# Two-layer adapter and mixture kernel: first layer in steps of two groups, expert numbers read two slots ahead

## What is computed

```python
# layer 0: per batch a 64x64 mixing matrix, then a router over 8 experts of rank 16, the best two
z = einsum('bct,bcd->bdt', x, W0[id0])                 # mixes the 64 rows of a batch
w = top-2 gates of softmax(z @ router_w.T + router_b)  # 8 experts
x = x + einsum('ner,eor->no', (z @ A.T) * w, Bm) * 0.5
# layer 1: per batch one of 16 adapters (1024x1024), a base product, 16 experts of rank 64, the best two
y = einsum('bij,bkj->bik', x, W1[id1])
x = x + y @ base_w.T + base_b + 0.5 * sum_e gate_e * (y @ A1.T) @ B1[e].T
```

## Time and profile before

| | us |
|---|---|
| median of three runs | 1165.05 (1164.32 to 1165.34) |
| the profiled execution | 1167.17 |
| its span | 1165.6 |
| PE busy in it | 1103.1 (95%) |
| DVE busy | 686.3 (59%) |
| ACT busy | 505.3 (43%) |
| POOL busy | 222.2 (19%) |

### The profile page before, as it was taken

One profiled execution on the slowest core, in us unless ns is written; L12 is line 12 of the kernel. 1 busy time (PEld: TensorE's weight loads), 2 busy tenths in 40 slices (PEclk: granted clock), 3 DMA queues, 4 the chain that ended last, 5 costly groups with the idle time before them and its releaser, 6 DMA issues.

```text
span 1165.6 us, 22333 instructions
## 1 busy us (share of the span) xinstructions
PE 1103.1 (95%) x5801; PEld 916.3 (79%) x5802; DVE 686.3 (59%) x1321; ACT 505.3 (43%) x1027; POOL 222.2 (19%) x354
## 2 busy tenths in 40 slices
PE   4899979999999899999999999999999999999998
PEld 4899967878778687878878878767777778888886
DVE  4788943563755637463565486834455366566666
ACT  1012213563745637453565462134555444444443
POOL 1111110020201102010111000054545232223210
PEclk9899979999999899999999999999999999999999
DMA  6499765493765729475665432169999899999995
GB/s 212 169 313 326 258 223 177 136 323 114 256 222 195 266 82 325 153 259 180 221 221 183 137 102 88 57 223 330 345 336 334 315 404 341 348 354 337 324 323 204
DMA packets 114925, 283.11 MB, mean 243 GB/s; under 512 B 17202, under 2 KB 22322, under 8 KB 112946
## 3 DMA queue, kind: packets, MB, share of 16 engines
q1 hardware_dynamic: 85232, 178.95, 43.3%
q0 software_dynamic: 29216, 102.91, 26.0%
q10 hardware_dynamic: 418, 0.53, 0.2%
HBM read 181.65 MB, written 100.70 MB: 242 GB/s over the span
## 4 chain that ended last, share of the span: by engine, by line
PE 74%; DVE 11%; issue 4%; DMA 4%; ACT 3%; DVEq 1%; SPq 1%; ACTq 1%; POOL 0%; POOLq 0%; another core or an unknown queue 0%
PE psum L1439 18%; PE psum L1441 17%; PE psum L1440 17%; PE psum L1533 3%; PE psum L1637 3%; PE psum L1636 3%; PE psum L1525 2%; PE psum L1645 2%; DVE x1g L1045 2%; PE psum L1534 2%; PE psum L1551 2%; PE psum L1553 1%; DMA xp<-act_scratch 1%; PE psum L1449 1%; ACT w L821 1%
## 5 line engine op out<-in xcount | busy, mean ns | idle before, releaser
L1439 PE MATMUL psum<-base_hi,xp_hi 128*128 128x512 f32 x512 | 207.6, 405 | 6.2 <-DVE xp_lo L1177 3.4
L1441 PE MATMUL psum<-base_hi,xp_lo 128*128 128x512 f32 x512 | 200.4, 391 | 0.0
L1440 PE MATMUL psum<-base_lo,xp_hi 128*128 128x512 f32 x512 | 200.2, 391 | 0.0
L1439 PE MATMUL psum<-w,xp_hi 128*128 128x512 f32 x448 | 182.8, 408 | 6.3 <-DVE xp_lo L1095 3.2
L1441 PE MATMUL psum<-w,xp_lo 128*128 128x512 f32 x448 | 177.7, 397 | 0.0
L1440 PE MATMUL psum<-w,xp_hi 128*128 128x512 f32 x448 | 177.3, 396 | 0.0
L1077 DVE TENSOR_TENSOR w<-raw,w 128x1024 fp32r<-128x1024 f32 x112 | 132.4, 1221 | 29.5 <-ACT w L758 23.6
L639 POOL DMA_DIRECT2D raw<-w1T x112 | 59.4, 530 | 442.8 <-DVE w L1077 417.5
L803 ACT ACTIVATE xp_hi<-xp 128x256 fp32r<-128x256 f32 x124 | 51.6, 418 | 183.1 <-PE psum L1441 152.3
L1439 PEld LDWEIGHTS psum<-base_hi,xp_hi 128*128 128x128 f32 x512 | 96.2, 188 | 39.8 <-issue 15.6
L1177 DVE TENSOR_TENSOR xp_lo<-xp,xp_hi 128x256 fp32r<-128x256 f32 x124 | 51.9, 424 | 119.3 <-ACT xp_hi L803 96.5
(11 more groups left out here) (278 smaller groups left out, 1993.5 us busy)
## 6 DMA issues: line engine op xcount, KB each, us to landing
raw<-w1T POOLq DMA_DIRECT2D x120, 512.0 KB, 5.6
delta_scratch<-dl SPq DMA_DIRECT2D x80, 512.0 KB
xp<-act_scratch SPq DMA_DIRECT2D x74, 256.0 KB, 3.3
act_scratch<-yT SPq DMA_DIRECT2D x72, 256.0 KB, 2.2
act_scratch<-x1g SPq DMA_DIRECT2D x16, 1024.0 KB, 5.3
x1t<-act_scratch SPq DMA_DIRECT2D x64, 256.0 KB
out<-x1t SPq DMA_DIRECT2D x62, 256.0 KB
xg<-xT SPq DMA_DIRECT2D x15, 1024.0 KB, 8.6
```

The costliest lines, as they stand in the source:

```text
L1439: mm(out, a_hi, b_hi, start=start, stop=False, skip_group_check=True)
L1440: mm(out, a_hi, b_lo, start=False, stop=False, skip_group_check=True)
L1441: return mm(out, a_lo, b_hi, start=False, stop=stop, skip_group_check=True)
```

## The change

Groups are taken in steps of two (`NS` = 8 steps). `gates0(n)` does both groups of a step in one chain of 17 instructions on tensors twice as wide, and then four products into `hw0`; the y products have two banks (1 and 7), so the index tables move to bank 6; the ring of x has six places, two of them in memory that the second layer uses later. PE, ACT and SP are written out without loops. SP loads `w0tab` behind the first group and ahead of the second (before: ACT, after the first half of the first group had landed). `index_3`, `index_sums(4)` and a new `index_read` (three reads of bank 6) run before the first gates, the rest of `index_4` behind them. In the last steps gates, turns and adds are ordered by hand. POOL waits for 12 groups of `x1_added` before it loads the first pair. The expert numbers are multiplied by `D` on DVE, bounded there alone, and read two slots ahead.

```diff
@@ SP
             sp.dma_start(xg[0][:, ks, :], xT[0, :, ks, :]).then_inc(xg_first[q], 16)
+            for h in range(2):
+                sp.dma_start(w0tab[h * C:(h + 1) * C, :], w0).then_inc(w0_in, 16)
             load_x(1, 1)
@@ POOL
             pool.wait_ge(const_split, 2)
+            pool.wait_ge(x1_added, 4 * (2 * XRING))
@@ ACT
+            def two_groups(n):
+                act.wait_ge(shift0, n + 1)
+                act.activation(sm[:, 1, :, :], sm[:, 0, :, :], ACT.Exp).then_inc(exp0, 1)
+                act.wait_ge(h0T_done, n + 1)
+                for k in range(2):
+                    g = 2 * n + k
+                    if n > 0:
+                        act.wait_ge(o_done, 4 * (g - 2) + 4)
                     ...
+                    act.activation(h0_hi[:, rows_of_g], h0T_of(g), ACT.Copy).then_inc(h0_hi_done, 1)
             z_copy(0)
             ...
-            group0(0)
-            ...
-            with act.Fori(1, NG - KC - 1) as g:
-                group0(g)
+            z_copy(1)
+            z_copy(2)
+            for n in range(NS):
+                two_groups(n)
+                ...
+                for k in range(2):
+                    if 2 * n + 3 + k < NG:
+                        z_copy(2 * n + 3 + k)
+                    if n < NS - 1 and NS - 5 <= n:
+                        w_high(2 * (n - NS + 5) + k, 16)
@@ DVE
+            index_3()
+            index_read()
             gates0(0)
+            for n in range(NS - 1):
+                hidden_low(2 * n)
+                hidden_low(2 * n + 1)
+                if n == 0:
+                    index_4()
+                else:
+                    add_x(2 * n - 1, 1)
+                if n == NS - 2:
+                    gates0(n + 1)
+                add_x(2 * n, 0)
+                add_x(2 * n, 1)
+                ...
+                if n < NS - 2:
+                    gates0(n + 1)
+                    add_x(2 * n + 1, 0)
+                if NS - 5 <= n < NS - 2:
+                    w_low(0, 2 * (n - NS + 5))
+                    w_low(0, 2 * (n - NS + 5) + 1)
+            hidden_low(NG - 2)
+            add_x(NG - 3, 0)
+            add_x(NG - 3, 1)
+            hidden_low(NG - 1)
+            w_low(0, KC - 2)
+            add_x(NG - 2, 0)
+            add_x(NG - 2, 1)
+            w_low(0, KC - 1)
+            add_x(NG - 1, 0)
+            add_x(NG - 1, 1)
@@ PE
+            def two_groups(n):
+                if n < NS - 1:
+                    turn_h0(n)
+                    z_of(2 * n + 3, 0)
+                    y_of(2 * n + 2)
+                    z_of(2 * n + 3, 1)
+                    ...
+                    y_of(2 * n + 3)
+                expand(2 * n)
+                if n == NS - 2:
+                    turn_h0(n + 1)
+                expand(2 * n + 1)
+                if n < NS - 2:
+                    z_of(2 * n + 4, 0)
+                    z_of(2 * n + 4, 1)
             ...
             index_sums(3)
+            z_of(1, 0)
+            y_of(0)
+            index_sums(4)
+            z_of(1, 1)
+            y_of(1)
+            z_of(2, 0)
+            z_of(2, 1)
+            for n in range(NS):
+                two_groups(n)
@@ experts
-                return pe.value_load(etab[0:1, s:s + 1], min_val=0, max_val=E1 - 1)
+                return nc.values_load(etab[0:1, s:s + 1], engines=[mybir.EngineType.PE], min_val=0,
+                                      max_val=(E1 - 1) * D,
+                                      skip_runtime_bounds_check_because="VectorE bounds every entry to 15 * D")
-                    m = experts[:, bass.ds(e * D + h * 512, 512)]
+                    m = experts[:, bass.ds(e + h * 512, 512)]
-            e = expert_of(0)
+            ahead = [expert_of(0), expert_of(1)]
             for s in range(NX):
-                expert(s, e)
-                if s + 1 < NX:
-                    e = expert_of(s + 1)
+                expert(s, ahead.pop(0))
+                if s + 2 < NX:
+                    ahead.append(expert_of(s + 2))
```

More of the change, by code:

```diff
@@ L136, in build @@
         with ExitStack() as s:
-            xg = [sb(s, f"xg{i}", [P, KC, GR]) for i in range(RING)]
+            xg = [sb(s, f"xg{i}", [P, KC, GR]) for i in range(XRING - 2)]
             x1g = [sb(s, "x1g0", [P, GB, KC, C])]
@@ L222, in build @@
         raw_in = [sem(f"raw_in{i}") for i in range(KC)]
-        xg_in = [sem(f"xg_in{i}") for i in range(RING)]
+        xg_in = [sem(f"xg_in{i}") for i in range(XRING)]
         x1_out = [sem(f"x1_out{i}") for i in range(2)]
@@ L406, in _, with store_x @@
             sp.dma_start(bias[:, :], bias1).then_inc(const_in, 16)
-            def store_x(g, slot):
+            for g in range(4, XRING):
+                load_x(g, g)
+            def store_x(g):
                 sp.wait_ge(x1_added, 4 * g + 4)
[L410 to L419, removed]
+                sp.dma_start(x1s[g * GB:(g + 1) * GB, :, :].rearrange("b p (i c) -> p b i c", c=C),
+                             x1g[g % 2][:, :, :, :]).then_inc(x1_out[g % 2], 16)
+            for g in range(NG):
+                store_x(g)
+                if g + XRING < NG:
+                    load_x(g + XRING, g % XRING)
             for s in range(2):
@@ L607, in w0_blocks @@
                     w0_block(2 * t + s, s)
-            for g in range(RING):
+            for g in range(4):
                 if g >= 2:
@@ L1462, in first_z, with y_of @@
                     last.then_inc(z_done, 1)
-            def y_of(g, slot):
+            def y_of(g):
                 pe.wait_ge(z_copied, g + 1)
                 pe.wait_ge(blk_ready, 4 * g + 4)
-                if not (isinstance(g, int) and g == 0):
-                    pe.wait_ge(hw0_ready, 2 * g)
+                if g >= 2:
+                    pe.wait_ge(hw0_ready, GS * (g // 2))
                 for m in range(GT):
-                    last = mm(yz_ps[:, m, :], w0blk[slot % 2][:, m, :], zsb[:, m, :], start=True, stop=True)
+                    last = mm(yz_ps[g % 2][:, m, :], w0blk[g % 2][:, m, :], zsb[:, m, :], start=True, stop=True)
@@ L1471, in y_of, with expand @@
                 last.then_inc(yz_done, 1)
-            def group0(g, slot, last_group=False):
-                if not last_group:
-                    z_of(g + 1, (slot + 1) % RING, 0)
-                pe.wait_ge(hw0_ready, 2 * g + 2)
-                if not (isinstance(g, int) and g == 0):
-                    pe.wait_ge(h0_lo_done, g)
-                for m in range(GT):
-                    last = pe.transpose(h0T_ps[:, m * P:(m + 1) * P], hw0[:, m, :], ident[:, :])
-                last.then_inc(h0T_done, 1)
-                if not last_group:
-                    z_of(g + 1, (slot + 1) % RING, 1)
-                if isinstance(g, int) and g == 0:
-                    pe.wait_ge(const_split, 1)
+            def expand(g):
@@ L1492, in group0, with turn_h0 @@
                         last = split_product(o, b0_hi[:, i * P:(i + 1) * P], b0_lo[:, i * P:(i + 1) * P],
-                                             h0_hi[:, :], h0_lo[:, :], i % 2 == 0, i % 2 == 1)
+                                             h0_hi[:, hs], h0_lo[:, hs], i % 2 == 0, i % 2 == 1)
                     last.then_inc(o_done, 1)
-                    if q == 0 and not last_group:
-                        y_of(g + 1, slot + 1)
+            def turn_h0(n):
+                pe.wait_ge(hw0_ready, GS * (n + 1))
+                if n > 0:
+                    pe.wait_ge(h0_lo_done, 2 * n)
+                for m in range(GS):
+                    last = pe.transpose(h0T_of(2 * n + m // GT)[:, m % GT * P:(m % GT + 1) * P], hw0[:, m, :],
+                                        ident[:, :])
+                last.then_inc(h0T_done, 1)
```

187 lines of the change are left out of this document (86 added, 101 removed).

## The result

| | us |
|---|---|
| median of four runs, before | 1164.68 (1164.16 to 1165.34) |
| median of four runs, after | 1180.57 (1175.56 to 1181.45) |
| ratio | 1.0129, interval 1.0107 to 1.0151 |
| the profiled execution, after | 1181.45, its span 1179.8 |

A forecast was written before the change was run, and what follows sets the result against it. PE, busy 95% of the span, was taken as the bound. 1167.2 + 8.4 (last add) + 8.5 (clock falls) + 1.0 (end holes) - 3.0 (experts) = 1182.1; the median lies 2.1 lower: 1180.0 us, 8-in-10 range 1169 to 1191.

The forecast's parts named there:

- Start: First layer's beginning: index tables now stand ahead of the first gates, so the first turn comes at 30.6 us.
- One step: First layer: two groups take PE 15.35 us against 15.56 before, a gain of only 0.2 us a step.
- The hole: Before each first-layer turn: Exp waits behind z_copy(2n+4) on ACT, leaving PE empty 2.8 us, or 3.85 in three steps.
- The end of the layer: First layer's last expansions: DVE sets the pace, last add at e + 18.5, or 166.9 us, 8.4 later at full clock.
- The clock: First layer: five of seven holes bring a fall of PE's clock at 1.7 us, 8.5, plus 1 for end holes.
- Experts: Experts' slots: without register operations and check, and with earlier reads, they end 3.0 us sooner, bounds 0 and 5.
- A second layer that starts sooner behind its last store: Second layer's start: coming sooner behind its last store than before would show the prediction wrong; no size given.
- No gap: First-layer steps: Exp isn't held by the copy of z(2n+4), steps take 15.35 us, time 1150; chance 0.08.
- The clock holds: First layer: PE's clock stays full through most gaps, time 1170.5, to 1173 with one or two falls; chance 0.22.
- The clock falls at each gap: First layer: the clock falls at all seven gaps and returns late, 3.4 us each, time 1194; chance 0.07.
- The ids aren't read earlier: Experts' slots: the load itself blocks PE's sequencer, 3 us more on any case, 1183; no separate chance given.

The follow-up runs named there:

- hole filled with work: Changed kernel with 10 to 14 useless PE products between z(2n+4) and the turn, Exp's order kept: 1170.76 us, ratio 1.0024 to the kernel before.
- The first experiment: Changed kernel with Exp(n+1) ahead of the second copy, z_copy(2n+4), instead of behind it: 1156.51 us, ratio 0.9904 to the kernel before.
- the kernel with the shorter wait: Changed kernel with Exp(n+1) still behind z_copy(2n+4), but ahead of the w_high between them in three steps: 1174.67 us, ratio 1.0060.
- the two kernels on top of the best one: Changed kernel with Exp ahead of the second copy, plus second-layer constants behind step 1's gates: 1155.14 us; also last w_low before group 14's adds: 1157.05 us.

## Why the prediction was right, step by step

The time predicted was 1180.0 and the time measured 1180.57. Against the profiled execution the sum was 1182.1, and it was 1181.45. Not all of this closeness is earned, since one term was too small and two small ones were missing. The hole and its cause were right and are most of the result. But the slots were off by 5.6 us to one side, and the two terms put at nothing by 5.5 to the other: that these cancel is luck.

| part | predicted | measured |
|---|---|---|
| last add, full clock | 166.9 | 166.2 (hole filled with work) |
| falls of the clock and holes at the end | 9.5 | 9.7 (175.9 less 166.2) |
| last add to the first slot | 0 | +3.4 (613.0 against 609.6) |
| the slots | -3.0 | -8.6 (141.6 against 150.2) |
| behind the slots | 0 | +2.1 (249.3 against 247.2) |
| span | +14.9 | +14.2 |

**Start.** The first turn was forecast at 30.6 and came at 31.4.

**One step.** The work of PE was forecast at 15.35, and 15.3 to 15.7 are measured once the hole is gone, 15.66 in the steady part. The gain of 0.2 us a step that the prediction took from it did not come. y(2n+3) stands directly behind its copy, as said:

```profile
95.60 0.73 PE L1506 MATMUL psum<-zsb,w0blk 128*128 128x136 f32 x4 [0.49 <-ACT zsb L692]
```

**The hole.** It was forecast at 2.8 and 3.85 us, 2.5 and 3.5 in records; the records show 2.48 and 3.42. The waits from 25 to 175 us have it as PE's largest (total, times, longest):

```profile
PE psum L1528 <- DVE hw L1052: 22.4, 8, 3.4
```

The periods at full clock are 17.98 and 18.93, against 18.15 and 19.2 of the sum. Of that difference 0.09 is DVE's start behind Exp's end (86.69 to 86.79, against 0.19 in the sum), and another 0.11 is `w_high`, which holds Exp for 0.94 (106.12 to 107.06) and not 1.05.

ACT's strict order, which the prediction took from the earlier trace rows and from the Trainium skill (TensorE: Matmul & The Clock Gate, section on the array's architecture), is what the rows show: Exp never passes the copy, though its input is ready 5.5 us earlier. The first experiment shows that nothing else held it.

**The end of the layer.** Forecast e + 18.5. The first of the four last expansions starts at 157.87, and the last add ends at 175.9, so 18.05. DVE's timeline has the order that was forecast, `w_low`, the short wait for the ring's store, adds, `w_low`, adds:

```profile
168.40 1.22 DVE L1076 TENSOR_TENSOR w<-raw,w 128x1024 fp32r<-128x1024 f32 x1
169.88 2.48 DVE L1070 TENSOR_TENSOR x1g<-psum,xg 128x512 f32<-128x512 f32 x4 [0.27 <-DMA act_scratch<-x1g]
172.28 1.22 DVE L1076 TENSOR_TENSOR w<-raw,w 128x1024 fp32r<-128x1024 f32 x1
173.41 2.48 DVE L1070 TENSOR_TENSOR x1g<-psum,xg 128x512 f32<-128x512 f32 x4
```

**The clock.** Five falls of 1.7 were forecast for the seven holes, and 1 us more for the holes at the end. The trace has six of 1.67: five in the six periods from the first turn (only the second period, the one from 50.99, had none), and one behind the seventh turn, at 150.41:

```profile
150.00:155.00 5.00, 4.59 (x25) 4.59 (x26) 5.00 (x10) 0.66 (x2) 0.00 (x0) 0.66 0.01 2
```

Behind the hole of 2.10 us ahead of the last turn the clock stayed at 1.00, so the 1 us stood for something that did not come. Six falls make 10.0; the first turn is 0.3 us earlier than in the kernel with the hole filled, and that leaves the 9.7 of the table. So the price of a fall was right, the count was one too low and the extra term covered it. The count was a choice between bounds of 0 and 24 us, made from two rows that pointed in opposite ways, and that the sum of 9.5 fits is in part luck.

**Experts.** This term was mis-sized. The prediction had 3.0 with an upper bound of 5, from the longer records of one product and its idle time. The edit alone gives 6.3 us at the median (0.54% of 1165; 3.8 to 8.7 by the interval), and 8.1 in the slots of its profile. The bound was wrong because it was made from the longer records of one product (81 of 47 ns) and not from the starts. Taken from the starts, the time over PE's pace of 0.234 us a product sums to 16.0 us in the slots before and to 8.1 with the edit alone; the step up to the product behind the load gives 3.0 us of that back, and the step behind it, where the prediction had nothing, 2.8. Single profiles vary: in the nine with the check left out the slots take 143.7 us on average (141.6 to 145.0), in the three that keep it 149.3 (147.4 to 150.3). So the 8.6 of the table holds some 3 us of chance, and 5.6 is the better size.

**What offset it.** Ahead of the second pair's first product PE stands 4.05 us, where before it stood 1.67, and then it begins the pair at half speed. The record, and the windows around it:

```profile
194.17 0.76 PE L1474 MATMUL psum<-w,xp_hi 128*128 128x512 f32 x1 [4.05 <-DVE xp_lo L1130]
```

```profile
190.00:194.00 4.00, 0.12 (x1) 0.00 (x0) 0.69 (x1) 1.73 (x4) 0.00 (x0) 0.80 1.03 409
194.00:200.00 6.00, 5.83 (x18) 4.67 (x19) 2.76 (x6) 1.25 (x3) 0.00 (x0) 0.56 0.78 299
```

Before, the same stretch ran at full speed:

```profile
177.00:183.00 6.00, 6.00 (x31) 4.98 (x30) 4.05 (x8) 3.21 (x7) 0.00 (x0) 1.00 0.67 260
```

18 products in 6 us against 31 in as many, at 0.19 us each: about 2.5 us of the 3.4; the other 0.9, and why the wait is longer, are open. "A second layer that starts sooner behind its last store" was named as a sign of error and did not come: the pair's first product starts 18.3 us behind the last add, and 18.2 before.

Behind the slots the clock fell once more, right behind a wait of 2.2 us; DVE, for which PE waits there, had waited for the gather. Before, a wait of 2.0 left it at full speed:

```profile
945.00:955.00 10.00, 7.80 (x35) 6.18 (x35) 7.13 (x9) 3.69 (x12) 3.94 (x5) 0.83 1.03 407
```

A mean of 0.83 over 10 us is half speed for 3.4, or 1.7 us of the 2.1. The kernel with Exp moved loses more in the same place: a wait of 4.1 us and a clock of 0.67, and 251.5 us behind the slots against 247.2.

```profile
925.00:935.00 10.00, 8.96 (x36) 7.64 (x37) 5.43 (x7) 3.50 (x12) 3.75 (x4) 0.67 1.03 403
```

This is where part of the gain of that kernel went. Its last add is 8.7 us earlier and its slots are 5.3 us shorter, 14.0 together, but its span only 8.4. Of the 5.6 given back, 4.3 are lost behind the slots and 1.3 ahead of them. Why the gather comes late there in one run and not in another is open.

**The rivals.** "No gap" was forecast at 1150. With Exp moved the ratio of 0.9904 is 1153.9 on the scale of 1165.05. Its last add ends at 149.8 against the forecast 146.4; 1.7 of these 3.4 us are the constants' long period, 0.9 the later start and 0.9 the three periods of 15.66. "The clock holds" was forecast at 1170.5, and with the hole filled the ratio of 1.0024 gives 1167.8; the 2.7 between them are the size of the experts' error. "The clock falls at each gap" came close in the count, six of seven, and not in the price: each fall cost 1.67 and not 3.4. "The ids aren't read earlier" can be told more exactly now: reading them earlier has no worth of its own that could be measured.

## What to carry to other kernels

When steps are made larger in a kernel with one hand-written stream an engine, list for each short instruction that others wait for (here an Exp of 0.22 us) what now stands ahead of it in its own stream and when that can run at the earliest; a copy of 0.4 us ahead of it cost 2.5 us a step, and turned a kernel that could be 1% faster into one 1.3% slower. A hole in PE's stream has two prices, its length and the fall of the clock behind it, and filling it with products that nobody uses tells them apart. The number of falls could not be forecast here; a forecast should carry it as a range. In the experts' slots the register check directly behind each load was worth 0.4%, and a load one slot earlier nothing that could be measured, with the check (1.0013) or without it (0.9946 against 0.9965).

## What the runs showed of the hardware

- A fall of the granted clock costs 1.67 us each time in the steps of the first layer (15.01 to 16.68 us for 124 products). Behind holes of 2.5 us in PE's records it came three times in four in the changed kernel, and behind every second of seven, three times, in the kernel with the shorter wait; behind holes of 3.4 us it came all three times. Behind the hole of 2.1 us ahead of the last turn it came in the kernel with the shorter wait and in the two kernels on top of the best one, but not in the changed kernel, nor with Exp moved, nor with the hole filled. So a hole of the same length can go either way, which is why the count could not be read from the trace of before. Behind the slots a hole of 2.0 us left the clock at 1.00 in the kernel before, and behind one of 2.2 us it fell in the changed one.
- A register check of 151 + 18 ns right behind each load (566 ns in the median) costs 5 to 6 us over 80 slots, although the starts of two slots lie 1.9 us apart. Leaving out the check brings this back (0.9956); reading one slot earlier does not (1.0013).
